# Three PSUM banks for T and three for S in the first attention layer, in place of two and four

## The reference

```
q, k, v = heads(x @ Wq.T), heads(x @ Wk.T), heads(x @ Wv.T)      # 4 x 16 heads, 1024 x 8
scores  = where(causal, -inf, q @ k.T / sqrt(8))
out     = softmax(scores) @ v, merged over the heads, @ Wo.T
```

## Time and profile before

| | |
|---|---|
| time, median of 3 runs | 2335.16 us (2334.02 to 2335.99) |
| profiled execution | 2343.62 us |
| its span, first to last instruction | 2341.9 us |
| PE busy | 2097.0 us, 90% |
| DVE busy | 1542.6 us, 66% |
| ACT busy | 1373.8 us, 59% |
| POOL busy | 487.9 us, 21% |

### The profile page before, as it was taken

How to read it: one execution, slowest core, us unless ns; L and a number is a source line. 1 busy time by engine, 2 the same in 40 slices (tenths; PEclk the granted TensorE clock), 3 DMA queues, 4 the chain that set the end, 5 groups by cost and what they waited for, 6 DMA issues and landing times. The chain is left out here.

```text
span 2341.9 us, 43593 instructions
## 1 busy us (share of the span) xinstructions
PE 2097.0 (90%) x10732; PEld 1351.8 (58%) x10732; DVE 1542.6 (66%) x6216; ACT 1373.8 (59%) x2513; POOL 487.9 (21%) x808
## 2 busy tenths in 40 slices
PE   3479999999963999999977999999999997499998
PEld 2245555555533788888733555555555547378886
DVE  4378778877825677777755666666666633567776
ACT  1236666666653889999842555555555565355554
POOL 4101111111103000000000111111111110266665
PEclk9779999999995999999986999999999998599999
DMA  3533334333301221122166555555555521076552
GB/s 95 175 51 54 53 46 60 51 50 50 46 22 63 55 55 37 37 45 45 18 234 186 127 118 117 117 121 128 128 128 117 117 46 58 25 157 120 132 122 60
DMA packets 96650, 202.81 MB, mean 87 GB/s; under 512 B 14496, under 2 KB 32160, under 8 KB 96032
## 3 DMA queue, kind: packets, MB, share of 16 engines
q1 hardware_dynamic: 96544, 201.65, 38.8%
HBM read 169.47 MB, written 31.60 MB: 86 GB/s over the span
## 5 line engine op out<-in xcount | busy, mean ns | idle before, releaser
L575 DVE CUSTOM_DVE_ANT_0 a1ms<-a1S,mask_q 128x128 bf16<-128x128 f32 (+1 forms) x758 | 387.8, 553 | 182.6 <-issue 179.1
L629 ACT ACTIVATE a1p<-a1T 128x512 f32<-128x512 f32 x576 | 331.4, 597 | 293.9 <-PE a1T L731 293.4
L575 DVE CUSTOM_DVE_ANT_0 a0ms<-a0S,mask_q 128x384 bf16<-128x384 f32 (+2 forms) x752 | 379.7, 553 | 109.6 <-issue 108.2
L629 ACT ACTIVATE a0p<-a0T 128x512 f32<-128x512 f32 x576 | 330.0, 597 | 188.7 <-PE a0T L731 177.8
L710 PE MATMUL a1O<-a1p,a1v 128*33 128x512 f32 (+3 forms) x1536 | 304.3, 496 | 1.0 <-POOL a1p L543 0.9
L731 PE MATMUL a0T<-a0qT,a0kT 128*128 128x512 f32 (+3 forms) x768 | 265.4, 392 | 18.3 <-DMA a0qT<-a0mr 6.8
L1184 DVE TENSOR_TENSOR m_hl<-m_h,m_hh 128x512 fp32r<-128x512 f32 x288 | 197.7, 690 | 116.8 <-ACT m_hh L1140 111.7
L731 PE MATMUL a1T<-a1qT,a1kT 97*128 97x512 f32 (+3 forms) x768 | 262.8, 390 | 0.7 <-DMA a1qT<-a1mr 0.7
L670 PE MATMUL a0S<-a0kS,a0qS 128*128 128x384 f32 (+2 forms) x752 | 229.0, 361 | 27.9 <-DMA a0kS<-scr_k 21.7
L731 PEld LDWEIGHTS a1T<-a1qT,a1kT 97*128 97x128 f32 x768 | 131.6, 189 | 200.7 <-ACT a1p L629 144.5
L670 PE MATMUL a1S<-a1kS,a1qS 96*128 96x128 f32 (+1 forms) x758 | 220.6, 353 | 13.0 <-DMA a1kS<-scr_k 12.8
(11 more groups left out here) (234 smaller groups left out, 3628.3 us busy)
## 6 DMA issues: line engine op xcount, KB each, us to landing
m_gb<-scr_g SPq DMA_DIRECT2D x48, 1024.0 KB, 8.6
a1qS<-scr_q SPq DMA_DIRECT2D x96, 256.0 KB, 6.1
a1qT<-scr_q SPq DMA_DIRECT2D x96, 256.0 KB, 4.0
a1kS<-scr_k SPq DMA_DIRECT2D x96, 128.0 KB, 6.8
a1kT<-scr_k SPq DMA_DIRECT2D x96, 128.0 KB, 4.7
scr_q<-p_hi SPq DMA_DIRECT2D x32, 256.0 KB, 2.5
scr_q<-p_lo SPq DMA_DIRECT2D x32, 256.0 KB, 2.7
a0qS<-scr_q SPq DMA_DIRECT2D x48, 128.0 KB
```

The source lines that it names most:

```text
L575: nc.vector.tensor_tensor_reduce(masked_s[spare][:, 0:c1 - c0], buf[:, 0:c1 - c0], k.mask_q[:, SEQ - w + c0:SEQ - w + c1], 1.0, NEVER, ALU ...
L629: nc.scalar.activation(prob_of(g, p)[:, h, :], t_ps[slot % 2][:, :], ACT.Exp, scale=scale)\
```

## The change

`attention` gets an argument TBUF, the number of T banks; S gets (6 - TBUF) x HALVES / 2. Layer 0 is called with TBUF = 3: three banks for T, three for S, two for the output. Layer 1 keeps two, four and two.

```diff
-def attention(..., PARTS=1, BURST=1, HALVES=2):
+def attention(..., PARTS=1, BURST=1, HALVES=2, TBUF=2):
...
-    BANKS = 2 * HALVES
+    BANKS = (6 - TBUF) * HALVES // 2
+    assert 2 * NSLOT % TBUF == 0
...
-        t_ps = [... (name + f"T{i}", [P, ST], F32)) for i in range(2)]
+        t_ps = [... (name + f"T{i}", [P, ST], F32)) for i in range(TBUF)]
...
-    nc.scalar.activation(prob_of(g, p)[:, h, :], t_ps[slot % 2][:, :], ACT.Exp, scale=scale)\
+    nc.scalar.activation(prob_of(g, p)[:, h, :], t_ps[(g[1] * NSLOT + slot) % TBUF][:, :], ACT.Exp, scale=scale)\
...
-    if not (at(g, 0) and slot < 2):
-        pe.wait_ge(exp_done, lin(g, NSLOT, slot - 1))
+    if not (at(g, 0) and slot < TBUF):
+        pe.wait_ge(exp_done, lin(g, NSLOT, slot - TBUF + 1))
...
-        last = nc.tensor.matmul(t_ps[slot % 2][:, off:off + q1 - q0],
+        last = nc.tensor.matmul(t_ps[(g[1] * NSLOT + slot) % TBUF][:, off:off + q1 - q0],
...
-    unit(units_from([("o", 0, 0, 0)]), before(END)[HALVES:], main_ring(unit_slot(END) + HALVES), n, END)
+    unit(units_from([("o", 0, 0, 0)]), (before(END) + units_of(END))[HALVES:], main_ring(unit_slot(END) + HALVES), n, END)
...
-              load_v0, attn)
+              load_v0, attn, TBUF=3)
```

More of the change, by code:

```diff
@@ L323, in _, with attention @@
                 pipelined(pe, NST // 2, front, back)
-def attention(k, name, HG, VD, scale, operands, load_q, load_k, load_v, out, PARTS=1, BURST=1, HALVES=2):
+def attention(k, name, HG, VD, scale, operands, load_q, load_k, load_v, out, PARTS=1, BURST=1, HALVES=2, TBUF=2):
     nc, sem = k.nc, k.sem
@@ L422, in attention @@
         s_ps = [c.enter_context(nc.psum_tensor(name + f"S{i}", [P, WIDTH], F32)) for i in range(BANKS)]
-        t_ps = [c.enter_context(nc.psum_tensor(name + f"T{i}", [P, ST], F32)) for i in range(2)]
+        t_ps = [c.enter_context(nc.psum_tensor(name + f"T{i}", [P, ST], F32)) for i in range(TBUF)]
         o_ps = c.enter_context(nc.psum_tensor(name + "O", [P, SEQ], F32))
```

## The result

| | before | changed |
|---|---|---|
| median | 2338.51 us (7 runs, 2334.02 to 2344.51) | 2352.82 us (7 runs, 2348.13 to 2360.25) |
| profiled execution, span | 2341.9 us | 2350.3 us |

The changed kernel is slower: ratio 1.0064, 95% interval 1.0041 to 1.0087, which is 15 us (10 to 20). The forecast was 7.6. The direction and the mechanism were right, the size was half. Of all runs behind this document one was in a slower state (2458.15 us, a run of e4, at a mean granted clock of 0.82 where the others have 0.94); it counts in no number here.

What follows compares the result with a forecast made beforehand. TensorE leads, its turns paced by waits for exponentials and VectorE's hold on S banks. Steady groups 14.7 + 0.2, back edges -2.5, end -4.8 make +7.6 us on 2335.2: 2343, own range 2337 to 2350, whole range 2322 to 2355.

Steps and rivals of the forecast that it cites:

- The rule of the turn: Four slots ending in a values step: an S bank is free 0.74 after VectorE starts on 512 columns, streams 0.12 later.
- slots 32-35: Turn with two units sharing the last slot: last S blocks held, 4.17 to 4.64, +0.47 a group, the largest term.
- slots 8-11: Turn whose fourth to sixth S blocks are held for a bank: 3.47 to 3.78, +0.31 a group.
- The sum over steady groups: Layer 0 groups with a full set of S: +1.05 each, fourteen of them, +14.7 us.
- the back edges: Five groups behind the loop's back edge: VectorE's pause starts earlier, turn 4.51 to about 4.17, five times -2.5 in all.
- Slots 20-27: Two turns where the fourth T load is released sooner: -0.13 (slots 20-23) and -0.17 (slots 24-27) a group.
- The end: Last group and three turns before it, without S: fourth T goes sooner, -4.8; six turns with S add +0.2.
- A: Rival, faster: the fourth bank of S was idle cover, price per group -0.30 in place of +1.05; -11, 2324; chance 0.16.
- all five losses: Held S units in slots 8-11, 28-31, 0-3, 32-35 and 4-7: +0.31, +0.20, +0.15, +0.47, +0.22 a group.
- C: Rival, no change: losses near 0.84 per group in place of 1.35, 2335; chance 0.18.
- B: Rival, much faster: the gate on exponentials was all that held the turns; -40, 2295; chance 0.04.
- D: Rival, slower still: late S blocks leave VectorE empty during the values step, losses double; +18.9 more, 2362; chance 0.08.

Runs made afterwards that it cites:

- e4: The changed kernel with VectorE's maximum in layer 0 taken over only half of each S block; median 2318.5 us, ratio to the kernel before 0.9907.
- e1: The changed kernel's three banks for S, but T keeps two and one bank lies idle; median 2360.8 us, ratio to the kernel before 1.0084.
- e2: The changed kernel with TBUF=4, so two banks for S and four for T; median 2460.6 us, ratio 1.0513.
- e6: The changed kernel with the loop over the groups of layer 0 written out; median 2340.4 us, ratio 1.0002.
- e7: The kernel before with four groups in a round of the loop in place of two, both layers; median 2347.5 us, ratio 1.0029.
- e5: The kernel before with the loop over the groups of layer 0 written out; median 2329.1 us, ratio to the kernel before 0.9960.

## Why the prediction was right, and where it was short

**The time against the ranges.** 2352.8 lies inside the range that was given, 2322 to 2355, but above the forecast's own, 2337 to 2350. Of the 9.8 us above 2343, 3.3 are the kernel before, whose median over seven runs is 2338.51 and not 2335.16; the rest is the change.

**The rule of the turn held.** A bank is free 0.74 after VectorE starts on 512 columns; the turns worked out from that lie within 0.07 of the measured ones, except slots 32-35 and the turns behind a back edge. That VectorE's hold is the cause is shown by e4, which turns the sign, and by e1, which has the loss without the T bank. The buffers `masked_s` went from four to three with it, but in the main part nothing waits for them.

**The sum over steady groups.** The fourteen intervals from the first values step of one group to that of the next make 484.4 after and 465.9 before, 18.5 more. The forecast had 14.7 for turns without back edges. A steady group without a back edge lasts 33.92 against 32.84, +1.08 where I had +1.05, and group 0, whose items lie one slot otherwise, gives +1.28: 14 x 1.08 + 0.2 = 15.3. Within it slots 32-35 came out 0.18 shorter than worked out, and slots 8-11 0.07 longer. I had let T of slot 33 wait behind a maximum that in the new order was done; VectorE started at 1.12 of the turn (413.12 - 412.00), not at 1.31:

```profile
412.00 0.19 PEld L732 LDWEIGHTS a0T<-a0qT,a0kT 128*128 128x128 f32 x1 [0.22 <-issue]
...
413.12 0.69 DVE L576 CUSTOM_DVE_ANT_0 a0ms<-a0S,mask_q 128x512 bf16<-128x512 f32 x1 [1.15 <-issue]
```

One number of the working is wrong in itself: the sum comes to nothing at losses of 0.81 a group (1.35 - 7.6 / 14), not of 0.84.

**The step that failed is the back edges**: "so the pause starts earlier ... in place of the +0.15 above -0.50, five times -2.5". It was +3.2 (18.5 - 15.3), so 5.7 of the 6.7 us by which the forecast fell short of the attention's 14.3. I had the pause of VectorE start when it has finished its blocks. VectorE behind the same back edge, after, answers to the earlier trace rows:

```profile
416.08 0.55 DVE L576 CUSTOM_DVE_ANT_0 a0ms<-a0S,mask_q 128x384 bf16<-128x384 f32 x1
...
418.62 0.06 DVE L573 MEMSET a0held<- 128x1 f32 x1 [1.98 <-PE a0S L671]
```

VectorE indeed came earlier to the end of its blocks. But the pause got longer by as much, 1.98 in place of 1.33. What stayed is the distance from the values step before, which goes right behind the last S block: 418.62 - 415.48 = 3.14 after, 416.53 - 413.42 = 3.11 before. At the thirty back edges of the six kernels with two groups in a round it lies between 3.09 and 3.49, in 25 of them at 3.25 or less, though VectorE's last maximum ends 1.79 behind that step before, 1.16 after, 0.68 in e2 and 0.61 in e4. So the price of the branch runs from the moment the last unit is handed to VectorE, and whatever VectorE still has to do hides it. A start at 2.2 of the turn as before, and a ring of three, where the fourth block and not the fifth waits for the first, gives 2.2 + 0.86 and a turn of 4.9 by the rule. That is what the trace shows:

```profile
416.46 0.19 PEld L732 LDWEIGHTS a0T<-a0qT,a0kT 128*128 128x128 f32 x1 [0.86 <-issue]
...
419.41 0.19 PEld L671 LDWEIGHTS a0S<-a0kS,a0qS 128*128 128x128 f32 x1 [1.85 <-DVE a0held L573]
...
420.38 0.12 PEld L711 LDWEIGHTS a0O<-a0p,a0v 128*9 128x9 f32 x8
```

The nearly constant distance is what the rows show; that VectorE's sequencer runs ahead to the branch while its blocks are still worked off is only my reading of it.

**The clock was no term of mine, and is one.** Two of the five back edges were followed by a turn of 5.46 and 5.37 in place of 4.13. The windows view of the second, after; the last three columns are granted clock, DMA share and GB/s:

```profile
489.60:491.30 1.70, 1.70 (x10) 0.12 (x8) 0.92 (x9) 0.60 (x1) 0.78 (x2) 0.55 0.00 0
491.30:493.00 1.70, 1.70 (x8) 1.40 (x5) 0.41 (x2) 0.77 (x2) 0.00 (x0) 0.50 0.16 36
```

The granted clock is at half, 1.2 GHz, for 3.4 us, in one place 1.0 and in the other 1.1 us behind the end of a wait of TensorE's queue of 1.9 and 1.8 us for one bank. It cost 1.3 us each time, 2.6 in all. The other three back edges had waits as long (1.83, 1.85, 1.93) and kept the clock, so whether it falls behind such a wait is luck as far as these rows tell. The ring's own share at the back edges is 0.8: their turns last 4.90 in the mean in place of 4.57, less the 0.17 or so that slots 0-3 lose anywhere, five times. The two make 3.4, and the long turns of slots 32-35, 1.1 us before and 0.7 after, take 0.4 off: 3.0 where the sum has 3.2. In the kernel before no load for S waited over 1.5 (the longest in the earlier trace rows), and no turn of slots 4-7 was long. With the loop written out, e6 has no such turn.

**The gains came as worked out.** Slots 20-27 gave 0.09 + 0.17 a group, forecast 0.13 + 0.17. The end gave 4.3 (0.7 in group 14 together with its losses, 3.5 in group 15), forecast 4.6 net. Together with the above: 15.3 + 3.2 - 4.3 = 14.2, the attention's 14.3.

**The rivals.** A would have had all five losses vanish; they all came. C needed losses near 0.84; they were 1.35 (0.38 + 0.23 + 0.17 + 0.29 + 0.24, and 0.04 in slots 12-19). B read the gap in front of T as the bound. The gap did go, from 188 waits to 56, but it gave only the 7.5 us that e1 shows, less than the bank of S cost; in e4, where VectorE holds a bank for less, moving the same bank gave 18.0. The rule of the Trainium skill (Perfetto Trace Analysis, Identifying Performance Opportunities), by which a repeating gap can mean too little PSUM, agrees with e4 and not with the change. D had the losses double because VectorE would run empty. Between the blocks of a turn it didn't; with two banks, in e2, it stands still for 0.1 to 0.3 us at three places between the blocks of slots 28-31.

## What to carry to other kernels

A PSUM bank is worth the time that the writer would otherwise wait for its reader; count that for each ring of banks before moving a bank from one to another. On an in-order queue a gate removed in one place gives only the time up to the next gate in the same slot, and a bank held for the other ring was that gate. Look for the stretches where one of the two rings is idle and lend its banks there: that gave the gain of the third T bank at the end of the layer at no cost in the groups before.

## What the runs showed of the hardware, unexpected

- Behind a back edge VectorE resumes 3.1 to 3.5 us after the values step that follows the last S block, whatever it still had to do then, and the pause is seen only as far as its backlog is shorter than that: 1.33 us before, 1.98 after. In layer 1 the same loop, two groups a round, shows no cost at all.
- A body twice as long (e7) made the branch dearer, not only rarer: TensorE, which passed it unseen in a body of two groups (0.98 to the next T load), sent its next T load only after 4.10 and 3.66 us, and the clock was at 0.50 behind both; in layer 1 it cost 0.5 us and more at each of six back edges. Straight code over all groups (e5) has neither. Whether that is the fetching of the code was not tried.
- Behind a back edge, waits of TensorE's queue of 1.8 to 1.9 us were followed in two of five cases by 3.4 us at 0.50 of the clock, the two waits of that length in e1 in one case, and waits of 2.2 to 2.5 us in e2 in three of five. Nine waits of 1.5 to 2.6 us in e4, five behind back edges and four for a DMA, were not, and neither were the waits of up to 1.5 us in the kernel before and in e1. So the length of the wait alone doesn't decide it.
- The waits for the DMA of the next keys in slots 32-35 come and go from profile to profile (one in the kernel before, three in e5, nine in e4) and make up to 10.5 us, as much as the change itself.
